# Two attention layers over eight images: the second layer's work of image 6 spread over the pauses of image 7

## The chip, the cores and the metric

The kernel runs on one core of a Trainium2 chip. The metric is the device time of one execution in microseconds (us). Times are medians of repeated runs; the trace is that of one profiled execution of the same program.

## The reference, cut to what matters

The input x has 8 batches (images) of 16 x 16 tokens with 256 channels. Two layers follow each other, and each adds to its input what it makes of a group-normalised copy:

```
x = x + L0(gn(x))     # L0: linear attention with 16 heads along rows and along columns, two output matrices
x = x + L1(gn(x))     # L1: softmax attention along rows and along columns, with distance bias, then Wo
gn: mean and variance over groups of 8 channels x 256 tokens
L1: q, k, v = x Wq + bq, x Wk + bk, x Wv + bv
    row:    softmax(q k - gw * dist) v   over the 16 tokens of a row
    column: softmax(q k - gw * dist) v   over the 16 tokens of a column
    out = (row + column) Wo + bo
```

## The kernel before, in words

All five engines have instruction streams of their own, in order, joined by semaphores; there is no planner, so the order that is written is the order that is run. One loop over batches is software-pipelined: while batch b goes through layer 0 (`attention`, `project`), the second layer of batch b-1 is worked off in between. BATCHES is 8 and LAST is 7.

The second layer of a batch in the loop, called the blocked form here, has these steps. TensorE makes `project_t` (one folded query-key product, 12 matmuls), then `project_values` for both halves of the tokens (6 matmuls each, the folded value-output product). ScalarE copies t (`take_t`) and the values to `v_row` (`take_values`); VectorE makes a copy of t turned to columns (`turn_t`). The values are turned to columns by two DMA steps on SP's queue: `put_values` writes `v_row` to a buffer in device memory and `turn_values` reads it back as `v_col`, after the semaphore `v_stored`. TensorE makes `block_scores` (64 small matmuls), VectorE adds the biases (`take_scores`, `shift_logits`, the second part of which waits for `v_turned`), ScalarE takes `exponentials`, VectorE divides (`sum_raised`, `scale_raised`) and transposes the weights (`turn_weights`). TensorE makes `block_values` (32 small matmuls), VectorE adds the result to the residual (`sum_rows`, `sum_columns`) and transposes it (`turn_y`), and SP stores it with eight DMAs of 32 KB (`store_y`).

The last batch has no successor, so after the loop a straight piece of code ends layer 0 of batch 7 and runs its second layer in another, dense form: statistics (`bn_stats`, `group_mean`, `group_variance`, the coefficients `nbias`), normalised copies split in a high and a low part (`xn_hi`, `xn_lo`), t (lines 1470 to 1477, read out as `t_last`), values and scores (`last_values`, `last_scores`, line 1489), logits and maxima (lines 1055 to 1062), exponentials (lines 620 and 621), weights `attn` (lines 1067 to 1072), their transposes (line 1509), the weighted values (line 1516), and two stores of 128 KB that ScalarE issues (line 628). Between them stand the steps of batch 6's blocked form. Matmuls of the identity with itself (`keep_busy`, line 1110) fill TensorE's waits; their results are not used. Line 1501 puts the residual into the accumulating bank before the weighted values.

Before the change TensorE's order after the loop is: t of batch 6, values 0, transposes of layer 0's row output, values 1, the second `queries`, `block_scores`, transposes of the column output, `project_out`, the column output's product (line 1453), `keep_busy(7)`, mean, `keep_busy(4)`, variance, `keep_busy(8)`, `block_values` of batch 6, then t, values and scores of batch 7, the residual, `keep_busy(6)`, and the transposes and weighted values of batch 7. SP's order is: put values of 6, turn them, store batch 5, store batch 6.

```python
            put_values(LAST - 1)
            turn_values(LAST - 1)
            store_y(LAST - 2)
            store_y(LAST - 1)
            sp.wait_ge(stored, 16 * (BLOCKS * LAST + TT))
```

Of the kernel before, what the change touches and what calls it, by code (L numbers as in the profile page):

```python
# [8 lines left out]
ACT = mybir.ActivationFunctionType  # L9
# [4 lines left out]
P = 128  # L14
# [30 lines left out]
def build(nc, x, w_qkv0, w_out0, w_qkv1, w_out1, wq, bq, wk, bk, wv, bv, wo, bo, sigma, out):  # L45
    with ExitStack() as ctx:
# [113 lines left out]
        xt_first = attn  # L160
        vp_banks, pv_banks, last_pv_banks = [bank[6], bank[1]], [bank[0], bank[6]], [bank[4], bank[5]]
        last_vp_banks = [bank[6], bank[7]]
# [94 lines left out]
        def _(sp):  # L257
# [4 lines left out]

            def store_y(b, chunks=range(CC)):
                sp.wait_ge(out_ready, b + 1)
                for c in chunks:
                    for quad in range(QUADS):
                        sp.dma_start(block_of(out_dram, b, c, quad), y_blk[quad * QUAD:(quad + 1) * QUAD, c, :, :]).then_inc(stored, 16)
# [76 lines left out]
            with sp.Fori(2, BATCHES - 2) as b:  # L344
                batch(b, 2, 2)
            batch(BATCHES - 2, 2, 1)
            put_values(LAST - 1)
            turn_values(LAST - 1)
            store_y(LAST - 2)
            store_y(LAST - 1)  # L350
            sp.wait_ge(stored, 16 * (BLOCKS * LAST + TT))
# [75 lines left out]
        def _(act):  # L427
# [66 lines left out]

            def take_values(b, t):
                act.wait_ge(vp_ready, TT * b + t + 1)
                act.activation(v_row[:, t, :], vp_banks[t][:, 0:WIDE], ACT.Copy).then_inc(v_taken, 1)

# [91 lines left out]
            with act.Fori(1, BATCHES - 1) as b:  # L590
# [3 lines left out]
            take_even(LAST, 1)  # L594
            mask_kv(LAST, 0)
            take_t(LAST - 1)
            take_values(LAST - 1, 0)
            split_o(LAST, 1, [bank[0], None])
            take_values(LAST - 1, 1)
            take_even(LAST, 0)  # L600
            act.wait_ge(ot_ready, 2 * BATCHES)
            act.activation(by_axis(o_last[:, 0, :], 0), bank[3][:, 0:TOKENS].rearrange("p (s i) -> p s i", s=SIDE), ACT.Copy
                           ).then_inc(last_o_taken, 1)
            exponentials(LAST - 1)

# [7 lines left out]
            act.wait_ge(last_t_ready, 1)  # L613
            act.activation(t_last[:, 0, :], last_t_bank[0][:, 0:TOKENS], ACT.Identity, bias=c1[:, 0:1]).then_inc(last_t_taken, 1)
            for t in range(TT):
                act.wait_ge(vp_ready, TT * LAST + t + 1)
                act.activation(vp_last[:, t, :], last_vp_banks[t][:, 0:DIM], ACT.Copy).then_inc(last_v_taken, 1)
# [8 lines left out]
            for t in range(TT):  # L626
                act.wait_ge(last_y_ready, t + 1)
                act.dma_start(out_dram[LAST, t * P:(t + 1) * P, :], y_last[:, t, :]).then_inc(stored, 16)


        @block.vector
        def _(dve):
# [129 lines left out]

            def shift_logits(b):

                dve.wait_ge(blocks_taken, b + 1)
                dve.wait_ge(v_taken, TT * (b + 1))
                dve.tensor_tensor(logit[:, 0:TT, :], logit[:, 0:TT, :], v_row[:, :, DIM:DIM + 1].broadcast_to([P, TT, BLOCK]), ALU.add)
                dve.wait_ge(v_turned, 16 * TT * (b + 1))
# [73 lines left out]
            def project(b, has_prev, next_batches):  # L842
# [5 lines left out]
                if next_batches >= 2:  # L848
                    statistics(0, b + 2)
                if has_prev:  # L850
                    shift_logits(b - 1)
                    sum_raised(b - 1)
# [145 lines left out]
            with dve.Fori(2, BATCHES - 2) as b:  # L998
# [6 lines left out]
            mask_kv(LAST, 0)  # L1005
            turn_t(LAST - 1)
            split_o(LAST, 1, [bank[0], None])
            take_odd(LAST, 0)
            turn_y(LAST - 2)
            dve.wait_ge(ot_ready, 2 * BATCHES)  # L1010
            dve.tensor_copy(by_axis(o_last[:, 1, :], 0), bank[7][:, TOKENS:2 * TOKENS].rearrange("p (s i) -> p s i", s=SIDE)
                            ).then_inc(last_o_taken, 1)
            take_scores(LAST - 1, bank[0])
            dve.wait_ge(res_loaded, 16 * LAST)
# [12 lines left out]
            last.then_inc(stat_in[1], 1)  # L1027
            shift_logits(LAST - 1)
            spread(LAST)
            variance(LAST)  # L1030
            sum_raised(LAST - 1)
            scale_raised(LAST - 1)
            turn_weights(LAST - 1)
            coefficients(LAST)
# [10 lines left out]

            sum_rows(LAST - 1, last_pv_banks)
            dve.wait_ge(last_t_ready, 2)
            dve.tensor_scalar(t_last[:, 1, :], last_t_bank[1][:, TOKENS:2 * TOKENS], c1[:, 1:2], None, ALU.add).then_inc(last_t_taken, 1)
            sum_columns(LAST - 1, last_pv_banks)
            for t in range(TT):  # L1050
# [10 lines left out]
                dve.wait_ge(last_logits, 2 * t + 2)  # L1061
                dve.tensor_reduce(neg_max[:, 1, t:t + 1], log_col[:, t, :], AX.X, ALU.max, negate=True).then_inc(last_max, 1)
            for t in range(TT):
                if t == 1:
                    turn_y(LAST - 1)
                dve.wait_ge(last_exp, t + 1)
                dve.reciprocal(inv_sum[:, :, t], exp_sum[:, :, t]).then_inc(last_inverse, 1)
                dve.wait_ge(last_inverse, t + 1)
                dve.tensor_scalar(attn[:, t, :], exp_col[:, t, :], inv_sum[:, 1, t:t + 1], None, ALU.mult).then_inc(last_scaled, 1)
                dve.wait_ge(last_scaled, t + 1)  # L1070
                own = attn[:, t, t * P:(t + 1) * P]
                dve.scalar_tensor_tensor(own, exp_row[:, t, :], inv_sum[:, 0, t:t + 1], own, ALU.mult, ALU.add).then_inc(last_weights_ready, 1)
            for t in range(TT):
                dve.wait_ge(last_pv_ready, t + 1)
                dve.tensor_copy(y_last[:, t, :], last_pv_bank[t][:, 0:DIM]).then_inc(last_y_ready, 1)
# [3 lines left out]
        def _(pe):  # L1079
# [135 lines left out]

            def project_values(b, t):

                if t == 0:
                    pe.wait_ge(r_split, 2)
                product(vp_banks[t][:, 0:WIDE],  # L1220
                        [((xn_hi[1][:, c, t * P:(t + 1) * P], xn_lo[1][:, c, t * P:(t + 1) * P]),
                          (wvo_hi[:, c, :], wvo_lo[:, c, :])) for c in range(CC)]).then_inc(vp_ready, 1)
# [212 lines left out]
            project_t(LAST - 1)  # L1435
            project_values(LAST - 1, 0)
            transpose_output(LAST, 1, [bank[0], None])
            project_values(LAST - 1, 1)
            queries(LAST, 0)
            pe.wait_ge(o_lo_done, 2 * LAST + 1)  # L1440
            block_scores(LAST - 1, bank[0])
            pe.wait_ge(o_done, 2 * BATCHES)
            for c in range(CC):
                for t in range(TT):
                    last = pe.transpose((bank[3], bank[7])[c][:, c * TOKENS + t * P:c * TOKENS + (t + 1) * P],
                                        o_tok[:, 0, t, c * P:(c + 1) * P], ident[:, :])
            last.then_inc(ot_ready, 1)
            pe.wait_ge(v_taken, TT * LAST - 1)
            project_out(LAST, 1, last_y_bank)
            pe.wait_ge(last_o_taken, 2)  # L1450
            for m, (done, count) in enumerate(((y_half, 1), (y_ready, 1))):
# [93 lines left out]
```

## Time and profile before

| what | us |
|---|---|
| median of 3 runs | 221.05 (220.75 to 221.3) |
| the profiled execution, own time | 221.89 |
| its span, first to last instruction | 219.7 |
| TensorE busy in the span | 211.5 (96%) |
| VectorE, ScalarE, GpSimd busy | 161.6, 119.5, 44.5 |

The time is longer than the span by what lies around the first and the last instruction. A matmul stream is pipelined, and its ends are modelled, so a busy TensorE is not TensorE at its peak; the filling matmuls count as busy too.

### The profile page before, as it was taken

How to read it: one execution, taken by the hardware profiler on the slowest of the kernel's cores; microseconds unless marked ns; L12 is line 12 of the kernel's file. 1: busy time of each engine (PE TensorE's matmuls, PEld its weight loads, DVE VectorE, ACT ScalarE, POOL GpSimd, SP SyncE). 2: the span in 40 equal slices, each digit the busy share in tenths (PEclk: the TensorE clock that was granted, in tenths of full speed). 3: DMA queues.
4: the chain of work that ended last, by engine and by line, in shares of the span. 5: the costliest groups of instructions: out<-in, count | busy, mean ns of one | idle time of the engine just before them, and what ended most of it. 6: DMA issues, size and time to landing. Idle time of an engine off the chain costs nothing.

```text
span 219.7 us, 9124 instructions
## 1 busy us (share of the span) xinstructions
PE 211.5 (96%) x3718; PEld 180.7 (82%) x3718; DVE 161.6 (74%) x484; ACT 119.5 (54%) x263; POOL 44.5 (20%) x64
## 2 busy tenths in 40 slices
PE   8799799999989999999999999999999999989995
PEld 4447689889968988898979897998898888988983
DVE  5699769667766777688677876787877666857782
ACT  2375474288616872677356853696269625830350
POOL 7500131012401070106010420115010701103000
PEclk9999999999999999999999999999999999999999
DMA  6962420233232342244224422334221421014004
GB/s 220 375 110 70 98 46 0 96 113 60 64 112 97 56 106 80 96 96 96 82 85 108 96 72 84 118 63 106 96 96 17 119 89 66 3 61 86 3 0 96
DMA packets 45568, 19.41 MB, mean 88 GB/s; under 512 B 35568, under 2 KB 41200, under 8 KB 45552
## 3 DMA queue, kind: packets, MB, share of 16 engines
q1 hardware_dynamic: 43872, 17.02, 28.5%
q10 hardware_dynamic: 1680, 2.16, 2.8%
q8 instruction: 11, 0.18, 0.4%
q14 instruction: 5, 0.04, 0.1%
HBM read 7.36 MB, written 3.95 MB: 51 GB/s over the span
## 4 chain that ended last, share of the span: by engine, by line
PE 80%; DVE 10%; DMA 3%; ACT 3%; issue 2%; SPq 0%; POOL 0%; ACTq 0%; DVEq 0%; POOLq 0%
PE bank L1086 42%; PE bank L1159 7%; PE bank L1181 7%; PE bank L1258 6%; PE bank L1190 3%; PE bank L1237 2%; PE bank L1110 2%; DMA turned_values<-v_row 2%; DMA v_col<-turned_values 1%; PE bank L1114 1%; PE bank L1104 1%; PE bank L1099 1%; PE bank L1516 1%; DVE wqkv_lo L883 1%; DVE moments L673 1%
## 5 line engine op out<-in xcount | busy, mean ns | idle before, releaser
L454 ACT ACTIVATE k_v<-bank 128x512 f32<-128x512 f32 x32 | 19.1, 598 | 37.8 <-PE bank L1086 35.6
L465 ACT ACTIVATE kv<-bank,head_scale 128x256 f32<-128x256 f32 x64 | 25.1, 476 | 8.5 <-PE bank L1159 8.5
L367 POOL TENSOR_TENSOR xt_lo<-xn,xn_hi 128x256 fp32r<-128x256 f32 x14 | 13.2, 966 | 56.3 <-DVE xn_hi L725 56.3
L381 POOL TENSOR_TENSOR rstd<-var_eps,minus_half 128x4 f32<-128x4 f32 x8 | 8.1, 1018 | 69.8 <-DVE var_eps L714 69.8
L733 DVE TENSOR_TENSOR kv<-bank,block_mask 128x512 f32<-128x512 f32 x32 | 20.5, 682 | 0.8 <-PE bank L1159 0.7
L1181 PE MATMUL bank<-kv,q 64*32 64x128 f32 x1024 | 18.5, 274 | 1.0 <-DVE kv L733 0.7
L752 DVE TENSOR_TENSOR o_lo<-bank,o_hi 128x256 fp32r<-128x256 f32 x30 | 13.9, 508 | 7.5 <-ACT o_hi L480 7.3
L1159 PE MATMUL bank<-v_wide,k_v 64*32 64x128 f32 x1024 | 18.4, 273 | 0.0
L1159 PEld LDWEIGHTS bank<-v_wide,k_v 64*32 64x32 f32 x1024 | 14.4, 105 | 3.4 <-issue 2.5
L1181 PEld LDWEIGHTS bank<-kv,q 64*32 64x32 f32 x1024 | 14.2, 105 | 3.3 <-issue 1.4
L1086 PE MATMUL bank<-o_hi,wout_hi 128*128 128x256 f32 x60 | 16.9, 281 | 0.0
L744 DVE SCALAR_TENSOR_TENSOR o_tok<-bank,parity,o_even 128x256 f32<-128x256 f32 x32 | 13.9, 476 | 3.9 <-ACT o_even L475 3.9
L1086 PE MATMUL bank<-o_lo,wout_hi 128*128 128x256 f32 x60 | 16.7, 278 | 0.0
L1086 PE MATMUL bank<-o_hi,wout_lo 128*128 128x256 f32 x60 | 16.6, 277 | 0.0
L475 ACT ACTIVATE o_even<-bank,parity 128x256 f32<-128x256 f32 x32 | 13.5, 480 | 4.1 <-PE bank L1181 4.1
L480 ACT ACTIVATE o_hi<-bank 128x256 fp32r<-128x256 f32 x30 | 12.8, 505 | 4.8 <-PE bank L1190 4.8
L458 ACT ACTIVATE q<-bank 128x512 f32<-128x512 f32 x16 | 9.6, 602 | 8.9 <-PE bank L1086 6.9
L1086 PE MATMUL bank<-wqkv_hi,xn_hi 128*128 128x512 f32 x28 | 11.6, 413 | 0.0
L1086 PEld LDWEIGHTS bank<-o_lo,wout_hi 128*128 128x128 f32 x60 | 11.3, 188 | 0.3
L1086 PE MATMUL bank<-wqkv_hi,xt_hi 128*128 128x512 f32 x28 | 11.5, 412 | 0.0
L1086 PEld LDWEIGHTS bank<-o_hi,wout_hi 128*128 128x128 f32 x60 | 11.3, 188 | 0.3
L1086 PEld LDWEIGHTS bank<-o_hi,wout_lo 128*128 128x128 f32 x60 | 11.3, 189 | 0.0
(239 smaller groups left out, 584.5 us busy)
## 6 DMA issues: line engine op xcount, KB each, us to landing
v_wide<-k_v SPq DMA_DIRECT2D x61, 64.0 KB, 1.9
turned_values<-v_row SPq DMA_DIRECT2D x7, 258.0 KB, 2.7
v_col<-turned_values SPq DMA_DIRECT2D x14, 129.0 KB
x_blk<-in_x_dram SPq DMA_DIRECT2D x56, 32.0 KB, 1.8
x_kept<-x_chan SPq DMA_DIRECT2D x7, 256.0 KB, 2.3
x_res<-x_kept SPq DMA_DIRECT2D x7, 256.0 KB, 2.2
out_dram<-y_blk SPq DMA_DIRECT2D x56, 32.0 KB, 1.7
wqkv_in<-in_L_conv_w_qkv_dram ACTq DMA_DIRECT2D x2, 384.0 KB, 5.8
```

The source lines that it names most:

```text
L367: pool.tensor_tensor(turn_to(xt_lo[:, c, :]), turn_from(xn[0][:, c, :]), turn_from(xn_hi[0][:, c, :].bitcast(FP32)), ALU.subtract)
L454: act.activation(k_v[:, axis, :, t, :], src[:, :].rearrange("p (i d) -> p i d", i=2), ACT.Copy).then_inc(kv_taken, 1)
L465: last = act.activation(kv[axis][:, 1, :, :, :, head // 2, own].rearrange("p t c s e -> p (t c s) e"), kv_bank[1][:, :].rearrange("p (a e) ...
L475: act.activation(o_even[:, r, :, :], src[:, :, 0, :], ACT.Copy, scale=parity[:, 0:1]).then_inc(o_even_done, 1)
L480: last = act.activation(by_axis(o_hi[:, axis, c, :], axis), banks[1 - axis][:, c * TOKENS:(c + 1) * TOKENS].rearrange("p (s i) -> p s i", ...
L733: last = dve.tensor_tensor(kv[axis][:, 0, :, :, :, pair, :].rearrange("p t c s e -> p (t c s) e"), kv_bank[0][:, :].rearrange("p (a e) -> ...
L744: last = dve.scalar_tensor_tensor(o_tok[:, axis, :, :].rearrange("p t (c h a) -> p (t c) h a", c=CC, h=HALVES)[:, :, r, :], src[:, :, 1, : ...
L752: last = dve.tensor_tensor(by_axis(o_lo[:, axis, c, :], axis), banks[1 - axis][:, c * TOKENS:(c + 1) * TOKENS].rearrange("p (s i) -> p s i ...
L1086: last = pe.matmul(dst, a, b, start=(first and i == 0), stop=(final and i == len(passes) - 1))
L1159: last = pe.matmul(kv_bank[r][pair * PAIR:(pair + 1) * PAIR, first:first + P], k_v[rows, axis, 0, t, channels], v_wide[rows, axis, :, t, c ...
L1181: last = pe.matmul(qkv_bank[r][quad * QUAD:(quad + 1) * QUAD, to:to + 2 * FOUR], q[rows, axis, c, first:first + QUAD], kv[axis][rows, quad ...
L1258: last = pe.matmul(dst, values[rows, t, m * P:(m + 1) * P], weights_t[rows, (1 - axis) * TT + t, :], start=True, stop=True)
```

## The change

The steps of batch 6's blocked form are put at other places of the last batch's code. Values, block scores and block values move later on TensorE, with other banks. `take_t`, `turn_t` and `take_values` stand behind the layer-0 steps on ScalarE and VectorE. `shift_logits` is cut in two: `add_row_term` and the rest. On VectorE the logits, the sums, the transposed weights and the output of batch 6 are laid between the steps of batch 7, to behind its weights. On SP the store of batch 5 goes ahead of and between the two steps of turning the values. The last two of the eight stores of batch 6 are issued by ScalarE behind its own last store. The counts of filling matmuls go from 7, 4, 8, 6, 2, 2 to 5, 10, 4, 2.

```diff
-        vp_banks, pv_banks, last_pv_banks = [bank[6], bank[1]], [bank[0], bank[6]], [bank[4], bank[5]]
+        vp_banks, pv_banks, late_pv_banks = [bank[6], bank[1]], [bank[0], bank[6]], [bank[5], bank[3]]
+        late_vp_banks, late_s_bank, last_ot_bank = [bank[4], bank[5]], bank[7], [bank[3], bank[0]]
...
-            def store_y(b, chunks=range(CC)):
+            def store_y(b, chunks=range(CC), left=0):
...
-                    for quad in range(QUADS):
+                    for quad in range(QUADS - (left if c == CC - 1 else 0)):
...
+            store_y(LAST - 2, range(1))
             put_values(LAST - 1)
+            store_y(LAST - 2, range(1, CC))
             turn_values(LAST - 1)
-            store_y(LAST - 2)
-            store_y(LAST - 1)
+            store_y(LAST - 1, range(CC), FEW)
...
             take_even(LAST, 1)
             mask_kv(LAST, 0)
+            split_o(LAST, 1, [bank[0], None])
+            take_even(LAST, 0)
             take_t(LAST - 1)
-            take_values(LAST - 1, 0)
-            split_o(LAST, 1, [bank[0], None])
-            take_values(LAST - 1, 1)
-            take_even(LAST, 0)
             act.wait_ge(ot_ready, 2 * BATCHES)
...
-            exponentials(LAST - 1)
+            take_values(LAST - 1, 0, late_vp_banks)
+            take_values(LAST - 1, 1, late_vp_banks)
...
             act.activation(t_last[:, 0, :], last_t_bank[0][:, 0:TOKENS], ACT.Identity, bias=c1[:, 0:1]).then_inc(last_t_taken, 1)
+            exponentials(LAST - 1)
...
+            act.wait_ge(out_ready, LAST)
+            for quad in range(QUADS - FEW, QUADS):
+                act.dma_start(block_of(out_dram, LAST - 1, CC - 1, quad), y_blk[quad * QUAD:(quad + 1) * QUAD, CC - 1, :, :]).then_inc(stored, 16)
...
-            turn_t(LAST - 1)
             split_o(LAST, 1, [bank[0], None])
             take_odd(LAST, 0)
+            turn_t(LAST - 1)
+            dve.wait_ge(ot_ready, 2 * BATCHES)
+            dve.tensor_copy(by_axis(o_last[:, 1, :], 0), last_ot_bank[1][:, TOKENS:2 * TOKENS].rearrange("p (s i) -> p s i", s=SIDE)
+                            ).then_inc(last_o_taken, 1)
             turn_y(LAST - 2)
...
-            take_scores(LAST - 1, bank[0])
...
-            shift_logits(LAST - 1)
+            take_scores(LAST - 1, late_s_bank)
             spread(LAST)
             variance(LAST)
-            sum_raised(LAST - 1)
-            scale_raised(LAST - 1)
-            turn_weights(LAST - 1)
+            add_row_term(LAST - 1)
             coefficients(LAST)
...
-            sum_rows(LAST - 1, last_pv_banks)
+            shift_logits(LAST - 1)
             dve.wait_ge(last_t_ready, 2)
             dve.tensor_scalar(t_last[:, 1, :], last_t_bank[1][:, TOKENS:2 * TOKENS], c1[:, 1:2], None, ALU.add).then_inc(last_t_taken, 1)
-            sum_columns(LAST - 1, last_pv_banks)
+            sum_raised(LAST - 1)
+            scale_raised(LAST - 1)
...
+                if t == 0:
+                    turn_weights(LAST - 1)
             for t in range(TT):
                 if t == 1:
-                    turn_y(LAST - 1)
+                    sum_rows(LAST - 1, late_pv_banks)
...
+            sum_columns(LAST - 1, late_pv_banks)
+            turn_y(LAST - 1)
...
             project_t(LAST - 1)
-            project_values(LAST - 1, 0)
             transpose_output(LAST, 1, [bank[0], None])
-            project_values(LAST - 1, 1)
             queries(LAST, 0)
-            pe.wait_ge(o_lo_done, 2 * LAST + 1)
-            block_scores(LAST - 1, bank[0])
+            project_out(LAST, 1, last_y_bank)
             pe.wait_ge(o_done, 2 * BATCHES)
...
-            pe.wait_ge(v_taken, TT * LAST - 1)
-            project_out(LAST, 1, last_y_bank)
+            project_values(LAST - 1, 0, late_vp_banks)
             pe.wait_ge(last_o_taken, 2)
...
+            project_values(LAST - 1, 1, late_vp_banks)
+            block_scores(LAST - 1, late_s_bank)
+            group_mean(LAST)
+            keep_busy(5, ident, bank[3])
+            group_variance(LAST)
+            keep_busy(10, ident, bank[3])
+
             pe.wait_ge(v_taken, TT * LAST)
-            keep_busy(7)
-            group_mean(LAST)
-            keep_busy(4)
-            group_variance(LAST)
-            keep_busy(8)
-            block_values(LAST - 1, last_pv_banks)
-
             pe.wait_ge(blocks_taken, LAST)
...
-            pe.wait_ge(out_sum, LAST)
+            pe.wait_ge(last_logits, TT)
+            block_values(LAST - 1, late_pv_banks)
...
-            keep_busy(6)
+            keep_busy(4, ident, bank[6])
...
-                keep_busy(2)
+                if t == 0:
+                    keep_busy(2, ident, bank[6])
```

## Rows read from the trace of the kernel before

**Rows 1.** The cores: span and mean granted TensorE clock
```profile
core 0: 219.7 us, clock 1.000
```

**Rows 2.** The chain that ended last: start us, us, what
```profile
204.06 1.99 PE bank L1258 x32
...
213.20 0.44 PE bank L1509 x2
...
217.10 0.42 DVE q L1075
```

**Rows 3.** Timeline, 190 to 198 us: start, length, engine, line, tiles [idle before]
```profile
190.25 0.28 PE L1086 MATMUL bank<-wvo_hi,xn_hi 128*128 128x258 f32 x1
190.45 0.84 ACT L492 ACTIVATE t_row<-bank,c 128x256 f32<-128x256 f32 x2
190.97 0.60 PE L1190 MATMUL bank<-ident,o_tok 128*128 128x128 f32 x4
191.18 0.39 ACT L497 ACTIVATE v_row<-bank 128x258 f32<-128x258 f32 x1
191.32 0.88 DVE L827 TENSOR_SCALAR t_col<-bank,c 128x256 f32<-128x256 f32 x2 [0.70 <-ACT t_row L492]
191.32 0.36 PE L1086 MATMUL bank<-wvo_hi,xn_hi 128*128 128x258 f32 x1
192.22 1.16 PE L1181 MATMUL bank<-kv,q 64*32 64x128 f32 x64
193.43 0.84 ACT L475 ACTIVATE o_even<-bank,parity 128x256 f32<-128x256 f32 x2 [0.72 <-PE bank L1181]
195.56 0.63 DVE L1011 COPY o_even<-bank 128x256 f32<-128x256 f32 x1
196.74 1.89 PE L1453 MATMUL bank<-o_even,wout_in 128*128 128x256 f32 x8
```

**Rows 4.** Timeline of SP's queue and VectorE, turned values of batches 0 and 5
```profile
53.62 0.39 SPq L308 DMA_DIRECT2D turned_values<-v_row  x1
...
61.46 0.23 DVE L769 TENSOR_TENSOR logit<-logit,v_col 128x64 f32<-128x64 f32 x1 [1.41 <-DMA v_col<-turned_values]
...
170.29 0.38 SPq L308 DMA_DIRECT2D turned_values<-v_row  x1
...
176.68 0.23 DVE L769 TENSOR_TENSOR logit<-logit,v_col 128x64 f32<-128x64 f32 x1 [0.85 <-DMA v_col<-turned_values]
...
177.26 0.29 DVE L774 TENSOR_TENSOR logit<-logit,peak 128x128 f32<-128x128 f32 x1
```

**Rows 5.** Timeline of VectorE, 198 to 211 us
```profile
198.67 0.42 DVE L1018 TENSOR_TENSOR x<-bank,x_res 128x256 f32<-128x256 f32 x1 [0.34 <-PE bank L1453]
...
205.10 0.42 DVE L1044 TENSOR_TENSOR xn_lo<-xn,xn_hi 128x256 fp32r<-128x256 f32 x1
...
207.67 0.48 DVE L1048 TENSOR_SCALAR x_in<-bank,c 128x256 f32<-128x256 f32 x1 [0.83 <-PE bank L1477]
...
208.80 0.22 DVE L1052 TENSOR_SCALAR row_term<-bank,s 128x1 f32<-128x1 f32 x1
...
209.46 0.35 DVE L1055 SCALAR_TENSOR_TENSOR log_row<-bank,row_term,row_mask 128x128 f32<-128x128 f32 x1 [0.44 <-PE bank L1489]
...
210.31 0.41 DVE L1062 TENSOR_REDUCE neg_max<-log_col 128x1 f32<-128x256 f32 x1
```

**Rows 6.** Timeline: weights of batch 6 on VectorE, residual and filling on TensorE
```profile
202.29 0.27 DVE L780 TENSOR_REDUCE total<-raised 128x4 f32<-128x128 f32 x1
...
203.46 0.45 DVE L795 STREAM_TRANSPOSE weights_t<-spread_out 128x256 f32<-128x256 f32 x1
...
210.55 1.08 PEld L1501 LDWEIGHTS bank<-ident,k_v 128*128 128x128 f32 x8
...
211.54 1.42 PEld L1110 LDWEIGHTS bank<-ident 128*128 128x128 f32 x12
```

**Rows 7.** The last stores: SP's issues of batch 6; line 628 from 217.3 us
```profile
213.79 3.80 SPq L267 DMA_DIRECT2D out_dram<-y_blk  x8
...
DMA to landing us min/median/max: 1.7/1.7/1.7
```

More of the change, by code:

```diff
@@ L493, in take_t, with take_values @@
                 last.then_inc(t_row_taken, 1)
-            def take_values(b, t):
+            def take_values(b, t, banks=vp_banks):
                 act.wait_ge(vp_ready, TT * b + t + 1)
-                act.activation(v_row[:, t, :], vp_banks[t][:, 0:WIDE], ACT.Copy).then_inc(v_taken, 1)
+                act.activation(v_row[:, t, :], banks[t][:, 0:WIDE], ACT.Copy).then_inc(v_taken, 1)
             def attention(b, has_prev, has_next):
@@ L595, in _ @@
             mask_kv(LAST, 0)
+            split_o(LAST, 1, [bank[0], None])
+            take_even(LAST, 0)
             take_t(LAST - 1)
-            take_values(LAST - 1, 0)
-            split_o(LAST, 1, [bank[0], None])
-            take_values(LAST - 1, 1)
-            take_even(LAST, 0)
             act.wait_ge(ot_ready, 2 * BATCHES)
-            act.activation(by_axis(o_last[:, 0, :], 0), bank[3][:, 0:TOKENS].rearrange("p (s i) -> p s i", s=SIDE), ACT.Copy
+            act.activation(by_axis(o_last[:, 0, :], 0), last_ot_bank[0][:, 0:TOKENS].rearrange("p (s i) -> p s i", s=SIDE), ACT.Copy
                            ).then_inc(last_o_taken, 1)
-            exponentials(LAST - 1)
+            take_values(LAST - 1, 0, late_vp_banks)
+            take_values(LAST - 1, 1, late_vp_banks)
             act.wait_ge(coef_ready[1], BATCHES)
@@ L761, in take_scores, with add_row_term @@
                                   block_bias[:, :].unsqueeze(1).broadcast_to([P, SLOTS, BLOCK]), ALU.add).then_inc(blocks_taken, 1)
-            def shift_logits(b):
+            def add_row_term(b):
                 dve.wait_ge(blocks_taken, b + 1)
@@ L767, in shift_logits @@
                 dve.tensor_tensor(logit[:, 0:TT, :], logit[:, 0:TT, :], v_row[:, :, DIM:DIM + 1].broadcast_to([P, TT, BLOCK]), ALU.add)
+            def shift_logits(b):
                 dve.wait_ge(v_turned, 16 * TT * (b + 1))
@@ L850, in project @@
                 if has_prev:
+                    add_row_term(b - 1)
                     shift_logits(b - 1)
@@ L1005, in _ @@
             mask_kv(LAST, 0)
-            turn_t(LAST - 1)
             split_o(LAST, 1, [bank[0], None])
             take_odd(LAST, 0)
+            turn_t(LAST - 1)
+            dve.wait_ge(ot_ready, 2 * BATCHES)
+            dve.tensor_copy(by_axis(o_last[:, 1, :], 0), last_ot_bank[1][:, TOKENS:2 * TOKENS].rearrange("p (s i) -> p s i", s=SIDE)
+                            ).then_inc(last_o_taken, 1)
             turn_y(LAST - 2)
-            dve.wait_ge(ot_ready, 2 * BATCHES)
-            dve.tensor_copy(by_axis(o_last[:, 1, :], 0), bank[7][:, TOKENS:2 * TOKENS].rearrange("p (s i) -> p s i", s=SIDE)
-                            ).then_inc(last_o_taken, 1)
-            take_scores(LAST - 1, bank[0])
             dve.wait_ge(res_loaded, 16 * LAST)
@@ L1214, in project_t, with project_values @@
                 last.then_inc(t_ready, 1)
-            def project_values(b, t):
+            def project_values(b, t, banks=vp_banks):
                 if t == 0:
                     pe.wait_ge(r_split, 2)
-                product(vp_banks[t][:, 0:WIDE],
+                product(banks[t][:, 0:WIDE],
                         [((xn_hi[1][:, c, t * P:(t + 1) * P], xn_lo[1][:, c, t * P:(t + 1) * P]),
@@ L1444, in _ @@
                 for t in range(TT):
-                    last = pe.transpose((bank[3], bank[7])[c][:, c * TOKENS + t * P:c * TOKENS + (t + 1) * P],
+                    last = pe.transpose(last_ot_bank[c][:, c * TOKENS + t * P:c * TOKENS + (t + 1) * P],
                                         o_tok[:, 0, t, c * P:(c + 1) * P], ident[:, :])
             last.then_inc(ot_ready, 1)
-            pe.wait_ge(v_taken, TT * LAST - 1)
-            project_out(LAST, 1, last_y_bank)
+            project_values(LAST - 1, 0, late_vp_banks)
             pe.wait_ge(last_o_taken, 2)
```

## The prediction

> **What bounds the kernel now.** I read the cores first: the span is 219.7 us and the granted clock 1.000 throughout, the upper of the two levels, 2.4 GHz [rows 1]. Then the chain that ended last: in the loop it is TensorE nearly everywhere, so the loop, which the change leaves alone, is no subject. In the last 30 us it changes hands. The piece to see is the block values of batch 6, 1.99 us at 204.06, which stand on the chain ahead of t of batch 7; the end is TensorE from the transposes at 213.20 to VectorE's last copy, which ends at 217.52 [rows 2], that is 4.32 us after the transposes begin. Then the timeline, for what each engine has in its queue around the moved steps.
>
> The sum is made against the profiled execution, 221.89 us, 2.19 more than its span and 0.84 over the median of 221.05. I carry the change of the span over to the median.
>
> **Step 1, up to the product of line 1453.** Values 0 and 1 leave TensorE's way ahead of the second queries. The transposes start at 190.25 instead of 190.97 (0.72), and the queries, 0.90 behind values 1 at 191.32 [rows 3], get nearly all of that too; I take 1.5 of the 1.62 us, because a small start gap of the queries stays. Queries: 192.22 to 190.7. ScalarE's even parts end 2.05 after the queries' start (193.43 + 0.84) [rows 3], at 192.75. But ScalarE now has t behind them: 0.84, to 193.6; VectorE's turned t waits for that: 0.88, to 194.5; only then comes its copy of the column output, 0.63 [rows 3], to 195.15. So here t, moved back, is late next: the output's transposes are ready some 0.7 us before VectorE gets to them. Line 1453 starts at 195.2 instead of 196.74: 1.5 us won. VectorE's transposition of batch 5 (`turn_y`) comes next and is hidden by those matmuls, half of whose 1.89 us [rows 3] must pass before VectorE has a result to take; without that cover it would cost its own length.
>
> **Step 2, the statistics.** x1 and all that hangs on it is 1.5 earlier. Values 1 and the block scores now stand between line 1453 and the mean on TensorE; 6 matmuls and 64 small ones fill just the time of VectorE's statistics (values 1 took 0.90 with the gap behind them, and the block scores I bound by the 64 matmuls of the queries, 1.16 [rows 3]), so I cost them at nothing, 0.3 at most. The four logit operations leave VectorE's way there, and the block values TensorE's, 1.99 [rows 2]. VectorE therefore ends its normalised parts, before at 205.52, at 204.0 or earlier [rows 5], and the first half of t could follow at once.
>
> **Step 3, the wait that is new.** Behind these parts VectorE now has `shift_logits`, which waits for the turned values. Its queue holds the second half of `t_last` behind it, and TensorE's scores wait for that. When do the turned values land? Values 1 come behind line 1453, whose eight records take 1.7 us of TensorE's queue, first matmul at 196.9; `v_row` is copied 0.93 after the first matmul (190.25 to 191.18) in 0.39 [rows 3]: 198.25. SP has by then issued four stores of batch 5, from 195.9 on, 0.475 each (3.80 for eight [rows 7]): free at 197.8, so hidden by half a microsecond; if they were later they would cost one for one. From the put to VectorE's use of the turned values 6.39 us pass in batch 5, with the four other stores issued in between as the change has it, and 7.84 in batch 0 [rows 4]. I take 6.5, near the first, since the change copies its order of stores, and batch 0 had none of it: 204.8. Thus VectorE stands still for about 0.8 us, and the gain of step 2 beyond 1.5 goes there.
>
> From 204.8: logits 0.87 (176.68 to 177.55 [rows 4]), `t_last` 0.48 [rows 5], to 206.18. Then on VectorE the sums and scaled weights, 1.17 (202.29 to 203.46 [rows 6]), and the row term, 0.22 [rows 5], to 207.6; TensorE's scores in the same time, 1.31 (208.15 to 209.46 [rows 5]), to 207.5. The logits of batch 7 start at 207.6 instead of 209.46: 1.86 won.
>
> **Step 4, the softmax.** The first half's maxima end 1.26 after that start (209.46 to 210.72 [rows 5]), at 208.86; the turned weights, 0.45 [rows 6], end at 209.3. Only now can TensorE begin the block values, because they need these weights. It is idle from the end of its scores until then. Behind them in its queue stand the residual (0.99, 210.55 to 211.54) and `keep_busy(4)` (1.42 for six, so 0.95) [rows 6], and then the transposes of batch 7: 209.35 + 1.95 + 0.99 + 0.95 = 213.25, against 213.20 [rows 2]. VectorE's weights for them come at about 211.8 (213.20 less 1.86, and 0.45 for the turned weights between), so TensorE, not VectorE, now sets that point. The 1.86 us are all given back: block values of 2 us that stood ahead of t now stand ahead of the transposes, with no wait to hide in but one that began too early. The last copy ends 4.32 later, at 217.6.
>
> **Step 5, the stores.** VectorE hands out batch 6 later, behind both sums and the second half of the weights, but it began 1.9 earlier; SP has six issues instead of eight (2.85 us), and its last would have to start after 218.5 to matter. ScalarE issues its second 128 KB at 217.6 and behind it two stores of 32 KB. Before, the last issue of all began at about 217.55 and landed in 1.7 us [rows 7]. Now two more issues follow: 0.4 for the one ahead and 0.475 for the next (SP's spacing, the nearest row), so the last begins at 218.5. ScalarE's price for this shape isn't shown; between half of SP's and twice it the last begins 0.6 to 1.5 later. I take 0.85 with 1.7 to land. The landing could be 0.2 shorter or 0.5 longer.
>
> The Trainium skill ("Trainium Kernel Development and Optimization", Key Constraints) says that issuing DMAs from several engines only saves the sequencer's issue time, since all run on the same 16 engines. By that rule the two issues cost SP 0.95 us less and the move pays if SP ended last; by the rows here ScalarE ends last, and the saving is on the wrong queue.
>
> Sum: +0.05 (transposes) + 0.85 (issues) = **+0.9**: a span of 220.6, a profiled time of 222.8, a median of 221.95. A measurement of this kernel tells 0.3% (0.66 us) from no change. With VectorE's wait 0.3 either way, TensorE's steps 0.2 and the last issue and landing as above, this case alone spans 221.3 to 222.8.
>
> **Rivals.**
> *The values are in time, no change (0.26).* If they land by 204.0, 0.8 earlier than I take, or the last store lands early, the sum is +0.1 to +0.6: about 221.3. For it: the waits in the loop are short, under a microsecond in batch 5 [rows 4]. Against: the put can't be earlier than line 1453 allows.
>
> *VectorE sets the transposes, faster (0.14).* If block values, residual and filling take 2.45 us or less together behind the weights instead of the 3.9 of the rows, the transposes come with VectorE's own weights at 211.8, 1.4 earlier; with the 0.85 of the stores that is -0.55, and with values in time up to -1.35: 219.7 to 220.5. It decides at 211.8: is TensorE at the transposes by then or not. Against: these instructions are the same as before, in one queue.
>
> *The turned values are late (0.10).* With the 7.84 us of batch 0 [rows 4] they land at 206.1, and all behind follows: +0.9 + 1.3 = +2.2, 223.25.
>
> *The clock falls (0.03).* TensorE idles before the scores and before the block values, each close to a microsecond, where the filling was taken away. The granted clock of the trace is 1.000 through all pauses that it has [rows 1], so nothing here shows a fall; at 1.2 GHz the 3.9 us ahead of the transposes would take twice as long, 225.9. The Trainium skill ("TensorE: Matmul & The Clock Gate", HAM oscillation) speaks against gaps in TensorE's work, since they throttle its clock; by it the change risks this, and the trace can't tell how far.
>
> **How the numbers follow.** My case has 0.47: +0.9, 221.95. Chances: slower 0.60 (my case, late values, the clock), the same 0.26, faster 0.14. The range from 220.3 to 223.0 takes in my case and the no-change rival whole, and leaves out most of the faster rival below and the late values and the clock above, 2 in 10.
>
> **What would show it.** Right: VectorE's second `v_col` logit waits for DMA at about 204 to 205 us, and t's second half stands behind it; the block values start at about 209.3 behind the turned weights; the first transposes stay near 213.2; the last DMA issue is ScalarE's, near 218.5. Wrong: no wait at `v_col`, transposes at 212 or earlier released by VectorE's `attn`, an SP issue or a landing within 1.8 us of the last copy that ends the span.

## The result, and the profile after

The changed kernel takes 222.12 us (median) against 221.05: a ratio of 1.0048 with a 95% interval of 1.0032 to 1.0064, or 1.07 us slower. In two later comparisons, each against the kernel before on the same chip, the ratio was 1.0048 (1.0024 to 1.0071) and 1.0035 (1.0020 to 1.0051). The forecast was 221.95 us, slower.

The rows below are those of a second trace of the changed kernel, called after_again here, because in the first one the granted clock was at half for some 13 us between 25 and 40 us, long before the changed steps; the ratios leave out such executions, of which both kernels have a few. Line numbers have moved by some ten lines: 1086 is now 1097, 1110 is 1121, 1258 is 1269, 1453 is 1460, 1489 is 1496, 1501 is 1509, 1509 is 1517 and 1516 is 1525.

The cores of the changed kernel: span and mean granted clock.

```profile
core 0: 219.1 us, clock 1.000
```

The chain that ended last in the changed kernel, from the column output's product on (start us, us, what):

```profile
194.25 1.99 PE bank L1460 x8
...
196.99 0.40 ACT v_row L499
...
197.40 2.53 DMA turned_values<-v_row
...
200.64 3.03 DMA v_col<-turned_values
...
205.01 1.13 PE bank L1496 x4
...
207.71 0.25 issue
207.97 2.00 PE bank L1269 x32
209.97 1.09 PE bank L1509 x8
211.06 0.89 PE bank L1121 x8
211.95 0.22 PE bank L1517 x2
...
215.63 0.42 DVE q L1086
```

Read it against [rows 2]. There the block values, 1.99 us at 204.06, stand ahead of t of batch 7, and only a chain of TensorE and VectorE follows. Now two transfers are on the chain, the put and the turning of batch 6's values, and the block values, still 2.00 us, have moved to behind the scores; directly behind them come the residual, the filling and then the transposes. Nothing was saved of them. They are at another place of the same chain.

What the transposes of batch 7 wait for has changed with it. VectorE's first weights `attn`, before and now, and the first of the transposes now:

```profile
212.79 0.35 DVE L1072 SCALAR_TENSOR_TENSOR attn<-exp_row,inv_sum,attn 128x128 f32<-128x128 f32 x1
```

```profile
209.76 0.35 DVE L1081 SCALAR_TENSOR_TENSOR attn<-exp_row,inv_sum,attn 128x128 f32<-128x128 f32 x1
...
211.78 0.38 PE L1517 MATMUL bank<-ident,attn 128*128 128x128 f32 x2
```

Before, the weights were ready at 213.14 and the transposes began at 213.20 [rows 2]: VectorE set that point, and the last weight load of the filling had ended at 212.96 [rows 6]. Now the weights are ready at 210.11, and TensorE gets to the transposes 1.67 us later.

The timeline of VectorE, and of the queues that issue DMAs, in the changed kernel:

```profile
202.14 0.42 DVE L1050 TENSOR_TENSOR xn_lo<-xn,xn_hi 128x256 fp32r<-128x256 f32 x1
...
203.69 0.23 DVE L777 TENSOR_TENSOR logit<-logit,v_col 128x64 f32<-128x64 f32 x1 [1.14 <-DMA v_col<-turned_values]
...
204.48 0.48 DVE L1054 TENSOR_SCALAR x_in<-bank,c 128x256 f32<-128x256 f32 x1
...
206.25 0.35 DVE L1062 SCALAR_TENSOR_TENSOR log_row<-bank,row_term,row_mask 128x128 f32<-128x128 f32 x1
...
207.43 0.43 DVE L803 STREAM_TRANSPOSE weights_t<-spread_out 128x256 f32<-128x256 f32 x1
...
213.06 2.84 SPq L268 DMA_DIRECT2D out_dram<-y_blk  x6
...
214.26 2.19 ACTq L630 DMA_DIRECT2D out_dram<-q  x2
...
216.49 0.98 ACTq L633 DMA_DIRECT2D out_dram<-y_blk  x2
```

VectorE is done with its normalised parts at 202.56 and stands still for 1.14 us until the turned values are there; `t_last` (line 1054) waits behind, and TensorE's scores behind that. At the end ScalarE issues two stores after its own second one, until 217.47, when nothing computes any more.

The whole loop shifts by up to 1.2 us from trace to trace, and by 5 us in the first one of the changed kernel, so stages are compared from one mark, the first matmul of t of batch 6. It stands at 188.79 before and at 187.75 in after_again:

```profile
188.79 0.37 PE L1086 MATMUL bank<-xn_hi,g_hi 128*128 128x256 f32 x1
```

```profile
187.75 0.37 PE L1097 MATMUL bank<-xn_hi,g_hi 128*128 128x256 f32 x1
```

The table gives starts after that mark, each worked out from the timeline of its trace (the chain can show a matmul up to 0.2 us later), and for the last two columns the end of VectorE's last copy and the end of the span.

| trace | column product | turned values used | logits of 7 | block values | transposes of 7 | last copy ends | span ends |
|---|---|---|---|---|---|---|---|
| before | 7.95 | 11.42 | 20.67 | 15.26 | 24.41 | 28.73 | 30.91 |
| changed, first trace | 6.42 | 15.93 | 18.49 | 20.20 | 24.02 | 28.29 | 31.32 |
| after_again | 6.50 | 15.94 | 18.50 | 20.22 | 24.03 | 28.30 | 31.35 |
| after_third | 6.46 | 16.52 | 19.08 | 20.80 | 24.62 | 28.88 | 31.92 |

So 1.5 us are won up to the column product, 1.6 to 2.2 up to the logits of batch 7, and at the transposes it is -0.4 to +0.2: given back. From the last copy to the end it is 3.0 us instead of 2.2. What differs between the traces of one kernel is nearly all in one column, the turned values.

### The profile page after: what moved, and what is told of

Its sections match the earlier page's. It is cut to its first block, busy times and chain, and to the rows that moved or that the text cites. A ratio compares the mean times of both kernels' runs of the same rounds, so it can differ in the third digit from the quotient of the medians.

```text
span 224.7 us, 9092 instructions
## 1 busy us (share of the span) xinstructions
PE 215.6 (96%) x3702; PEld 184.1 (82%) x3702; DVE 161.9 (72%) x484; ACT 119.5 (53%) x263; POOL 44.4 (20%) x64
## 4 chain that ended last, share of the span: by engine, by line
PE 82%; DVE 10%; DMA 2%; ACT 2%; issue 1%; POOL 0%; SPq 0%; DVEq 0%; POOLq 0%
PE bank L1097 44%; PE bank L1170 7%; PE bank L1192 7%; PE bank L1269 6%; PE bank L1201 4%; PE bank L1248 2%; PE bank L1286 1%; DVE moments L678 1%; DMA v_col<-turned_values 1%; PE bank L1125 1%; DMA turned_values<-v_row 1%; PE bank L1525 1%; DVE wqkv_lo L892 1%; PE bank L1110 1%; PE bank L1115 1%
## 5 line engine op out<-in xcount | busy, mean ns | idle before, releaser
L1192 PE MATMUL bank<-kv,q 64*32 64x128 f32 x1024 | 19.3, 283 | 0.7 <-DVE kv L738 0.7
L1170 PE MATMUL bank<-v_wide,k_v 64*32 64x128 f32 x1024 | 19.2, 282 | 0.0
L1170 PEld LDWEIGHTS bank<-v_wide,k_v 64*32 64x32 f32 x1024 | 15.0, 108 | 3.4 <-issue 2.7
L1192 PEld LDWEIGHTS bank<-kv,q 64*32 64x32 f32 x1024 | 14.8, 109 | 3.1 <-issue 1.3
L1097 PE MATMUL bank<-wqkv_hi,xn_hi 128*128 128x512 f32 x28 | 12.1, 432 | 0.0
L1097 PE MATMUL bank<-wqkv_hi,xn_lo 128*128 128x512 f32 x28 | 11.5, 412 | 0.0
```

The source lines that it names most:

```text
L1097: last = pe.matmul(dst, a, b, start=(first and i == 0), stop=(final and i == len(passes) - 1))
L1170: last = pe.matmul(kv_bank[r][pair * PAIR:(pair + 1) * PAIR, first:first + P], k_v[rows, axis, 0, t, channels], v_wide[rows, axis, :, t, c ...
L1192: last = pe.matmul(qkv_bank[r][quad * QUAD:(quad + 1) * QUAD, to:to + 2 * FOUR], q[rows, axis, c, first:first + QUAD], kv[axis][rows, quad ...
```

## The experiments

Theory A is that of the prediction: the late turned values hold VectorE, TensorE's queue behind the turned weights sets the transposes, and ScalarE's trailing stores set the end. Theory B is that TensorE's clock falls in the gaps that the change opens. All edits but one are made to the changed kernel; ratios are against the kernel before on the same chip, and times are the ratio's excess of 221.05 us.

**after_again and after_third**: no edit.

> The changed kernel once more, for a profile to stand beside the others. Theory A (the change's early gain is given back in TensorE's queue behind the turned weights of batch 6, and ScalarE's two trailing stores add to the end): 0.9 to 1.1 us above the kernel before with the clock at 1.000 throughout the last 35 us, and VectorE waiting about 1.2 us for the turned values. Theory B (the time is lost because TensorE's granted clock falls somewhere): a run at full clock is no slower than before.

> The changed kernel again, to stand on the same chip as the next three. Theory A: 0.5 to 1.1 us above the kernel before.

Ratios of 1.0048 (+1.06 us) and 1.0035 (+0.77 us). The granted clock was 1.000 in all stretches of after_again and of after_third up to the last copy; means under 1.000, such as after_third's 0.996, come from the end of the program, where TensorE has nothing left to do. VectorE's wait was 1.14 us and 1.74 us. Theory B falls for the changed kernel: in after_again's comparison its five runs with a mean clock of 1.000 took 221.25 to 222.72 us, those of the kernel before 220.39 to 221.62.

**no_fill**: the filling ahead of the transposes is left out.

```diff
-            keep_busy(4, ident, bank[6])
```

> The four filling matmuls ahead of batch 7's transposes are taken out. Theory A: they stand on the path, so the transposes and the end come 0.95 us earlier, to about 0.1 us above the kernel before. Rival (VectorE's weights set the transposes): no change, 1.0 us above before. Rival (the filling holds up the clock): a granted clock below 1.000 in the last 12 us and a longer time.

Ratio 1.0019 (1.0004 to 1.0034): +0.42 us, 0.64 less than after_again in the same comparison. The chain of no_fill, at the same place:

```profile
208.70 2.00 PE bank L1269 x32
210.70 1.09 PE bank L1509 x8
211.79 0.22 PE bank L1516 x2
```

From the block values to the transposes it is 3.09 us instead of 3.98 (211.95 less 207.97): 0.89 gone, as much as the filling's row. VectorE's weights don't set the transposes. The clock didn't fall for it: 1.000 up to the last copy. The time gained less than the 0.95 expected. In this trace the stretch from the last copy to the end is 3.21 us instead of 3.05, which is 0.16 of the difference; the rest lies inside the interval.

**fill_8**: eight filling matmuls instead of four at that place.

```diff
-            keep_busy(4, ident, bank[6])
+            keep_busy(8, ident, bank[6])
```

> Eight filling matmuls instead of four ahead of batch 7's transposes. Theory A: 0.9 us more than the changed kernel, 1.4 to 2.0 us above the kernel before, since they stand on the path; with none of them it was 0.6 less. Rival (VectorE's weights set the transposes): no change against the changed kernel.

Ratio 1.0081 (1.0062 to 1.0100): +1.79 us, 1.02 more than after_third. The chain of fill_8:

```profile
208.51 2.00 PE bank L1269 x32
210.51 1.09 PE bank L1509 x8
211.60 1.79 PE bank L1121 x16
213.39 0.22 PE bank L1517 x2
```

The filling is 1.79 long on the chain instead of 0.89. Doubled or removed, it costs what it takes, so TensorE's queue is the bound there.

**stores_sp**: all eight stores of batch 6 go back to SP.

```diff
-            store_y(LAST - 1, range(CC), FEW)
+            store_y(LAST - 1)
...
-            act.wait_ge(out_ready, LAST)
-            for quad in range(QUADS - FEW, QUADS):
-                act.dma_start(block_of(out_dram, LAST - 1, CC - 1, quad), y_blk[quad * QUAD:(quad + 1) * QUAD, CC - 1, :, :]).then_inc(stored, 16)
```

> All eight stores of batch 6 go back to SP, ScalarE issues only its own two. Theory A: ScalarE's two stores behind its last one set the end; SP's eighth starts 0.6 us before the present last one, so the end comes 0.5 to 0.6 us earlier, 0.4 to 0.5 above the kernel before. Rival (SP's queue is the one to be relieved): SP's last issue comes 0.95 us later than now and the end with it, 1.3 us or more above before.

Ratio 1.0020 (1.0001 to 1.0040): +0.44 us, 0.62 less than after_again. In its timeline SP issues all eight, from 213.64 to 217.44, and the span ends 2.67 us after the last copy instead of 3.05:

```profile
213.64 3.80 SPq L268 DMA_DIRECT2D out_dram<-y_blk  x8
...
216.21 0.42 DVE q L1083
```

The trace shows 0.38 of the 0.62. Giving SP all eight again is cheaper than letting ScalarE issue two at the very end.

**before_trail**: this part of the change alone, in the kernel before.

```diff
-            store_y(LAST - 1)
+            store_y(LAST - 1, range(CC), FEW)
...
+            act.wait_ge(out_ready, LAST)
+            for quad in range(QUADS - FEW, QUADS):
+                act.dma_start(block_of(out_dram, LAST - 1, CC - 1, quad), y_blk[quad * QUAD:(quad + 1) * QUAD, CC - 1, :, :]).then_inc(stored, 16)
```

> The kernel before with one part of the change alone: its last two stores of batch 6 are issued by ScalarE behind its own last store. Theory A (these two issues end the program): the stretch from VectorE's last copy to the end grows from 2.2 to 3.0 us, 0.8 to 0.9 us above the kernel before. Rival (issuing from a second engine saves SP's time and costs nothing): no change.

Ratio 1.0048 (1.0030 to 1.0065): +1.06 us, as much as the whole change, which had +0.77 in the same comparison: the two issues alone account for the loss. The rows of before_trail: VectorE's last copy on the chain, and ScalarE's issues.

```profile
216.46 0.42 DVE q L1078
```

```profile
217.32 0.97 ACTq L631 DMA_DIRECT2D out_dram<-y_blk  x2
```

The span, 219.9 us, ends 3.02 us after that copy, against 2.18 in [rows 2] and the span of [rows 1]. The stretch grew by 0.84, as expected, and the interval of the ratio, 0.66 to 1.44 us, holds that. Up to the stores this code is that of the kernel before, so it is also a second trace of it: from the mark its transposes start at 24.44 and its last copy ends at 28.77, against 24.41 and 28.73.

**between**: ScalarE issues the two stores between its own two.

```diff
+                if t == 0:
+                    act.wait_ge(out_ready, LAST)
+                    for quad in range(QUADS - FEW, QUADS):
+                        act.dma_start(block_of(out_dram, LAST - 1, CC - 1, quad), y_blk[quad * QUAD:(quad + 1) * QUAD, CC - 1, :, :]).then_inc(stored, 16)
-            act.wait_ge(out_ready, LAST)
-            for quad in range(QUADS - FEW, QUADS):
-                act.dma_start(block_of(out_dram, LAST - 1, CC - 1, quad), y_blk[quad * QUAD:(quad + 1) * QUAD, CC - 1, :, :]).then_inc(stored, 16)
```

> ScalarE issues its two stores of batch 6 between its own two stores of batch 7 instead of behind them. Theory A: the last issue of all is then the store of batch 7's second half, 0.85 us earlier, and lands with it: 0.2 to 0.3 us above the kernel before. Rival (the order is free, the transfers themselves set the end): no change, 1.0 us above before.

Ratio 0.9982 (0.9962 to 1.0001): -0.40 us, better than expected. ScalarE's issues in its timeline:

```profile
215.48 0.42 ACTq L630 DMA_DIRECT2D out_dram<-q  x1
215.94 0.98 ACTq L634 DMA_DIRECT2D out_dram<-y_blk  x2
217.30 0.36 ACTq L630 DMA_DIRECT2D out_dram<-q  x1
```

The stores now fit in ScalarE's wait for the second copy, and the span, 219.4 us, ends 2.14 us after that copy: 0.9 less than with the stores behind it. From the mark the span ends at 30.81, 0.10 ahead of the kernel before, and the interval, -0.84 to +0.02 us, holds that. The remaining 0.3 to 0.6 us of the difference to the changed kernel's +0.77 to +1.06 is not explained by this trace; the changed kernel was not run in this comparison, whose chip was another one.

**put_late**: all eight stores of batch 5 stand ahead of the put.

```diff
-            store_y(LAST - 2, range(1))
+            store_y(LAST - 2)
             put_values(LAST - 1)
-            store_y(LAST - 2, range(1, CC))
             turn_values(LAST - 1)
```

> All eight stores of batch 5 stand ahead of the put of the values on SP, instead of four ahead and four behind. Theory A: the put comes 1.1 us later, VectorE's wait for the turned values grows from 1.2 to 2.3 us, and all behind it follows: 2.0 to 2.2 us above the kernel before. Rival (the turned values are hidden, the wait costs nothing): no change against the changed kernel, 1.0 us above before.

Ratio 1.0141 (1.0099 to 1.0183): +3.1 us, more than expected. SP's eight issues took until 11.30 after the mark, the put came at 11.35, 1.7 us later than in after_again, and the turned values came at 17.98, 2.0 later. In the traced run the clock fell too. TensorE's timeline in that run, and its stretches (start and end, length, busy time of PE, PEld, DVE, ACT, POOL, then the granted clock, DMA share and GB/s):

```profile
207.74 1.94 PE L1495 MATMUL bank<-xn,x_in 128*128 128x256 f32 x4 [2.60 <-DVE x_in L1053]
...
209.69 0.42 PE L1096 MATMUL bank<-wvo_lo,xn_hi 128*128 128x258 f32 x1
```

```profile
206.00:207.00 1.00, 0.00 (x0) 0.00 (x0) 0.52 (x3) 0.00 (x0) 0.00 (x0) 1.00 0.00 1
207.00:208.00 1.00, 0.26 (x1) 0.27 (x2) 0.96 (x4) 0.58 (x2) 0.00 (x0) 0.96 0.00 0
208.00:209.00 1.00, 1.00 (x3) 0.77 (x3) 0.90 (x4) 0.00 (x0) 0.00 (x0) 0.50 0.00 0
209.00:210.00 1.00, 1.00 (x5) 0.86 (x4) 0.22 (x1) 0.00 (x0) 0.00 (x0) 0.50 0.00 0
210.00:211.00 1.00, 1.00 (x6) 1.00 (x6) 1.00 (x5) 0.00 (x0) 0.00 (x0) 0.50 0.00 0
211.00:212.00 1.00, 1.00 (x5) 0.55 (x4) 0.61 (x3) 1.00 (x4) 0.00 (x0) 0.84 0.00 0
```

TensorE stood for 2.60 us waiting for `t_last`, and just after it had begun again the granted clock went to 0.50, the 1.2 GHz level, for some three microseconds: the four score matmuls took 1.94 us instead of 1.13. This run and one other, both with a mean clock of 0.989, took 225.27 and 225.61 us; three with 0.995 to 0.998 took 223.50 to 223.74, which is 1.8 to 2.0 above 221.7, the median of after_again's runs that count in its ratio. So the turned values are on the path, nearly one for one, and in two of these five runs a second price came on top. That the longer wait brought the clock down fits the order of the rows, but no run tests it by itself. The rival that the values are hidden falls.

**values_early**: both values of batch 6 ahead of the column output's product, the put ahead of the stores.

```diff
             project_values(LAST - 1, 0, late_vp_banks)
+            project_values(LAST - 1, 1, late_vp_banks)
...
-            project_values(LAST - 1, 1, late_vp_banks)
             block_scores(LAST - 1, late_s_bank)
...
-            store_y(LAST - 2, range(1))
             put_values(LAST - 1)
-            store_y(LAST - 2, range(1, CC))
+            store_y(LAST - 2, range(1))
             turn_values(LAST - 1)
+            store_y(LAST - 2, range(1, CC))
```

> Both values of batch 6 stand ahead of the column output's product (line 1460) on TensorE, and SP puts them before the stores of batch 5, so the turned values land about 2 us earlier, while x1 comes 0.5 us later. Theory A: VectorE no longer waits for the turned values, and t's second half is read out when TensorE has it, 0.3 us earlier than now: 0.6 to 0.9 us above the kernel before, with TensorE's idle time ahead of the scores shorter. Rival (the turned values are not what holds VectorE): the 0.5 us later x1 shows in full, 1.5 us above before.

Ratio 0.9987 (0.9970 to 1.0004): -0.29 us, 0.9 better than the near end of what was expected. VectorE's rows:

```profile
203.36 0.22 DVE L777 TENSOR_TENSOR logit<-logit,v_col 128x64 f32<-128x64 f32 x1
...
204.76 0.48 DVE L1054 TENSOR_SCALAR x_in<-bank,c 128x256 f32<-128x256 f32 x1 [0.54 <-PE bank L1484]
```

The wait for the transfer is gone; `t_last` waits for TensorE. It starts 16.43 after the mark, against 16.73 in after_again, but 17.31 in after_third, where the turned values came later. The expectation was worked out from after_again, one of the two traces of the changed kernel whose wait was short; part of the miss is that. From the mark the span ends at 31.07, still 0.16 behind the kernel before, where the ratio says 0.29 ahead. As with between, the changed kernel was not run in this comparison, and whether the other chip is the rest is not shown.

**residual_first**: the residual ahead of the block values.

```diff
-            pe.wait_ge(last_logits, TT)
-            block_values(LAST - 1, late_pv_banks)
             pe.wait_ge(x1b_ready, BATCHES)
             pe.wait_ge(var_ready[1], BATCHES)
...
+            pe.wait_ge(last_logits, TT)
+            block_values(LAST - 1, late_pv_banks)
             keep_busy(4, ident, bank[6])
```

> The residual matmuls of batch 7 stand ahead of the block values of batch 6 instead of behind them, in TensorE's wait for the turned weights. Theory A: that wait is about 0.5 us, so about 0.5 of their 1.1 us leaves the path: 0.5 to 0.6 us above the kernel before. Rival (the wait is needed by nothing and the queue is not the bound): no change, 1.0 us above before.

Ratio 1.0017 (1.0000 to 1.0033): +0.38 us. From the use of the turned values to the transposes it is 7.78 us instead of 8.09 in after_again, so 0.31 is shown by the trace. The wait that it fills was shorter than the half microsecond that I had taken: 0.25 us, the row marked issue on the chain of after_again. The time is nevertheless a little better than the 0.5 to 0.6 expected, in the same comparison as between and values_early.

**combined and split_5_3**: no_fill, between, residual_first and values_early together; then with three of batch 6's stores on ScalarE instead of two.

```diff
-            store_y(LAST - 1, range(CC), FEW)
+            store_y(LAST - 1, range(CC), 3)
...
-                    for quad in range(QUADS - FEW, QUADS):
+                    for quad in range(QUADS - 3, QUADS):
```

> The stores between, the residual first, the values early and no filling ahead of the transposes, together. Theory A: the four terms add up, 0.8 + 0.5 + 0.3 + 0.7 us less than the changed kernel, as far as VectorE's own weights allow: 0.8 to 1.2 us below the kernel before. Rival (the clock falls where the filling is gone): a granted clock under 1.000 in the last 15 us and a time not below the kernel before.

> The combined kernel (stores between, residual first, values early, no filling) with three stores of batch 6 on ScalarE and five on SP instead of two and six. Theory A: in the combined kernel SP's last issue ends the program, about 0.55 us behind ScalarE's; with five and three the two queues end within 0.2 us of each other: 0.7 to 1.0 us below the kernel before and 1.3 to 2.0 below the changed one.

Ratios of 0.9966 (0.9949 to 0.9983) and 0.9956 (0.9941 to 0.9972): 0.75 and 0.97 us below the kernel before, and in the second comparison 1.75 below the changed kernel. Both beat the kernel before. split_5_3 beats the changed kernel beside which it was run; combined was not run beside it. Of the times expected, combined just missed its near end, 0.8 below. From the mark, the transposes start at 22.44 and 22.45 instead of 24.41 before and the last copy ends at 26.77 and 26.79 instead of 28.73: 1.95 us won, about the 1.86 that the prediction had won at the logits and lost again. The span ends at 30.17 and 30.22, 0.7 less than before; 1.2 of the gain goes to the end, where batch 6's output now comes late. In combined SP's six stores of it are issued last, until 28.43; in split_5_3 it is ScalarE's own second store, held up behind three of them, until 28.36. The rows of split_5_3:

```profile
213.51 0.40 ACTq L630 DMA_DIRECT2D out_dram<-q  x1
213.94 1.49 ACTq L634 DMA_DIRECT2D out_dram<-y_blk  x3
215.47 0.47 ACTq L630 DMA_DIRECT2D out_dram<-q  x1
```

Moving one more store to ScalarE put its last issue 0.54 later (27.82 to 28.36) and SP's 0.49 earlier (28.43 to 27.94); the trace shows no gain of it, and the two ratios don't tell them apart.

## Why the prediction was right

**Step 1** gave 1.5 us up to the column product; the traces give 1.45 to 1.53. This was in part luck. I had the column output's transposes ready some 0.7 us before VectorE, held up by t, gets to them. The rows of after_again:

```profile
191.39 0.38 PE L1097 MATMUL bank<-o_hi,wout_hi 128*128 128x256 f32 x1 [0.45 <-DVE o_lo L757]
...
192.60 0.88 DVE L835 TENSOR_SCALAR t_col<-bank,c 128x256 f32<-128x256 f32 x2 [0.22 <-ACT t_row L494]
...
192.91 0.60 PE L1453 MATMUL bank<-ident,o_tok 128*128 128x128 f32 x4
...
193.55 0.64 DVE L1019 COPY o_even<-bank 128x256 f32<-128x256 f32 x1
```

VectorE is done with t at 193.48, 5.73 after the mark, where I had it (194.5 in the time of before, that is 5.71). But the transposes end at 193.51 and no earlier, because `project_out`, which the change puts ahead of them, first waits 0.45 us for `o_lo`; I had not seen that. So the moved t costs nothing of its own: TensorE is as late as VectorE, and the sum came out right with one of its two causes missing.

**Step 2** cost the values and block scores at nothing; x1 to VectorE's end of the normalised parts is 5.86 us (14.81 less 8.95) against 6.43 before (16.73 less 10.30), so they cost nothing. The 0.6 less fits the logits that left VectorE; no run tests that by itself.

**Step 3**, the new wait, was placed and priced about right: turned values at 204.8 in the time of before, that is 16.0 after the mark, and 15.93 to 16.52 in the traces. I took 0.8 us for VectorE's wait; it was 1.14 in after_again and 1.74 in after_third, since VectorE got there 0.4 earlier than I had allowed and the values came up to half a microsecond later. put_late shows that the wait is on the path; in values_early it is gone, and `t_last` comes 0.3 to 0.9 earlier.

**Step 4** forecast +0.05 at the transposes, measured -0.4 to +0.2; no_fill and fill_8 show that TensorE's queue is the bound, and VectorE's weights, the condition of the faster rival, are not. TensorE's idle time ahead of the block values, which I had at close to a microsecond, was 0.25.

**Step 5** was sized well: 0.85 forecast, 0.84 in before_trail and 0.85 to 0.87 in the traces of the changed kernel (3.03 to 3.05 less 2.18). By the Trainium skill ("Trainium Kernel Development and Optimization", Key Constraints) issuing from a second engine saves only issue time. The traces agree: eight issues take 3.80 us on SP in stores_sp and six 2.84 in after_again, and the two on ScalarE take 0.98. But the saving lands on the queue that isn't last, and stores_sp and before_trail show its price.

**The rivals.** The late values came in part, 0.5 us later than I took in after_third: the spread between the traces of the changed kernel lies in that column, and put_late priced it. The clock rival did not happen in the changed kernel, where TensorE's pause ahead of the scores was 0.47 us in after_again and 1.04 in after_third, both at 1.000; put_late shows that it was not far off. The Trainium skill ("TensorE: Matmul & The Clock Gate", HAM oscillation) warns of gaps without matmuls, but the ones it names are longer than the 2.60 us of put_late's trace, behind which the granted clock went to 0.50; the measurement goes further than the page.

The medians put the changed kernel 0.8 to 1.1 us above before, the marks 0.4 to 1.0. Most of that gap can be put down to which execution was traced. Eight traces have the same code up to the turned values (the three of the changed kernel, no_fill, fill_8, stores_sp, between and residual_first); they use them at 15.93 to 16.52 after the mark, 16.3 in the middle, and the two traces with 0.4 are the two earliest. At 16.3 all that follows is 0.4 later than in after_again, which makes about 0.8. What stays open is the comparison of between, values_early and residual_first, whose times are 0.25 to 0.45 us lower than their marks say.

## What to carry to other kernels

Work that is moved into a pause has to be ready at that pause: here its weights came when the pause was nearly over, so two microseconds of matmuls only changed their place on the chain, and a filling that had ended before VectorE's weights came became part of the path. Before a DMA round trip is brought near a wait, compare its landing with the moment that the waiting engine arrives, and see what stands behind the waiting instruction in its queue. At the end of this program issues count, not bytes: each store costs its issuing engine about half a microsecond (0.45 to 0.55 for 32 KB, 0.36 to 0.47 for ScalarE's 128 KB), and in all fourteen traces the span ends 1.6 to 1.9 us after the last issue is done, whichever queue it is on.

## What the runs showed of the hardware

The round trip of the values through device memory, from the put's issue to VectorE's use, took from 6.29 us (after_again, 15.94 less 9.65) to 6.89 (after_third, 16.52 less 9.63), with the same instructions around it. And a wait of TensorE of 2.60 us was followed by a granted clock of 0.50 for three microseconds, just after the work had begun again, in the traced run of put_late (mean clock 0.989); pauses of up to 1.04 us behind the mark in the other traces left it at 1.000 up to the last copy. A second run had the same mean clock and nearly the same time; three others, with the same instructions, had 0.995 to 0.998 and were 1.5 us or more shorter, so the fall does not come each time. Nor does it need such a wait: in the first trace of the changed kernel the granted clock fell to 0.50 between 25 and 26 us, behind pauses of TensorE of about 0.7 us that after_again has at the same place, at 1.000.
